# Reading a matmul's 256 moving columns by turns from its two halves, in a non-local block on one core

## The reference, cut to what matters

```python
q = jnp.einsum('bchw,dc->bdhw', x, theta_w) + theta_b[None, :, None, None]     # 256 planes
xpool = _maxpool2(x)                                                          # 2 x 2, 256 pixels
k = jnp.einsum('bchw,dc->bdhw', xpool, phi_w) + phi_b[None, :, None, None]
v = jnp.einsum('bchw,dc->bdhw', xpool, g_w) + g_b[None, :, None, None]
qk = jnp.einsum('bdn,bdm->bnm', q, k) * hp ** (-0.5)
p = jax.nn.softmax(qk, axis=-1)
vp = jnp.einsum('bdm,bnm->bdn', v, p)
out = jnp.einsum('bdhw,cd->bchw', vp, z_w) + z_b[None, :, None, None]
return out + x
```

## Time and profile before

| | us |
|---|---|
| median of 3 runs | 2043.75 (2041.75 to 2043.93) |
| profiled execution, first to last instruction | 2040.4 |
| TensorE matmul rows, busy | 2026.8 |
| TensorE weight loads, busy | 2024.5 |
| VectorE busy | 1558.1 |
| GpSimd busy | 1366.5 |
| ScalarE busy | 1300.0 |

### The profile page before, as it was taken

One profiled execution on the slowest core, in us unless ns is written; L12 is line 12 of the kernel. 1 busy time (PEld: TensorE's weight loads), 2 busy tenths in 40 slices (PEclk: granted clock), 3 DMA queues, 4 the chain that ended last, 5 costly groups with the idle time before them and its releaser, 6 DMA issues.

```text
span 2040.4 us, 48999 instructions
## 1 busy us (share of the span) xinstructions
PE 2026.8 (99%) x17790; PEld 2024.5 (99%) x17790; DVE 1558.1 (76%) x2625; ACT 1300.0 (64%) x2228; POOL 1366.5 (67%) x828
## 2 busy tenths in 40 slices
PE   9999999999999999999999999999999999999998
PEld 9999999999999999999999999999999999999998
DVE  8878777787777877777877778777787777787777
ACT  6666666666566665666666666666666566666663
POOL 4577666776666766667766677666677666776663
PEclk9999999999999999999999999999999999999999
DMA  7565656746556565566565664656656556656554
GB/s 243 191 212 184 213 169 214 236 170 210 175 207 232 180 210 185 186 226 210 181 212 171 215 237 169 209 177 207 232 180 210 184 187 226 209 182 214 170 193 166
DMA packets 213963, 407.27 MB, mean 200 GB/s; under 512 B 12720, under 2 KB 17840, under 8 KB 213936
## 3 DMA queue, kind: packets, MB, share of 16 engines
q1 hardware_dynamic: 213792, 406.90, 59.0%
q10 hardware_dynamic: 144, 0.01, 0.0%
HBM read 272.64 MB, written 134.22 MB: 199 GB/s over the span
## 4 chain that ended last, share of the span: by engine, by line
PE 97%; DVE 2%; POOL 0%; DMA 0%; issue 0%; ACT 0%; SPq 0%; DVEq 0%; POOLq 0%
PE bank L967 97%; DVE x_top L755 0%; DVE pt_raw L736 0%; DMA x<-x 0%; DVE x_bot L755 0%; DVE pooled L708 0%; POOL att_lo L631 0%; POOL x_split_lo L613 0%; POOL att_f L626 0%; DVE x L755 0%; PE bank L974 0%; SPq L265 0%; DVE q_lo L714 0%; ACT att_hi L425 0%; DVE xp_lo L851 0%
## 5 line engine op out<-in xcount | busy, mean ns | idle before, releaser
L613 POOL TENSOR_TENSOR x_split_lo<-x,x_split_hi 128x1024 fp32r<-128x1024 f32 x255 | 614.6, 2417 | 248.4 <-ACT x_split_hi L386 226.7
L967 PE MATMUL bank<-x_split_hi,theta_hi 128*128 128x256 f32 x2048 | 565.8, 276 | 3.1 <-POOL x_split_lo L613 2.0
L967 PE MATMUL bank<-x_split_lo,theta_hi 128*128 128x256 f32 x2048 | 565.7, 276 | 0.0
L967 PE MATMUL bank<-x_split_hi,theta_lo 128*128 128x256 f32 x2048 | 565.7, 276 | 0.0
L967 PE MATMUL bank<-att_hi,z_hi 128*128 128x256 f32 x1792 | 495.4, 276 | 3.6 <-DVE x_bot L755 2.5
L967 PE MATMUL bank<-att_hi,z_lo 128*128 128x256 f32 x1792 | 494.9, 276 | 0.0
L967 PE MATMUL bank<-att_lo,z_hi 128*128 128x256 f32 x1792 | 494.9, 276 | 0.0
L736 DVE STREAM_TRANSPOSE pt_raw<-probs 32x256 f32<-32x256 f32 x1024 | 445.9, 435 | 18.4 <-ACT probs L489 1.8
L631 POOL TENSOR_TENSOR att_lo<-att_f,att_hi 128x768 fp32r<-128x768 f32 x191 | 282.6, 1487 | 159.4 <-ACT att_hi L425 159.4
L967 PEld LDWEIGHTS bank<-x_split_hi,theta_hi 128*128 128x128 f32 x2048 | 384.6, 188 | 3.5 <-issue 3.5
L967 PEld LDWEIGHTS bank<-x_split_hi,theta_lo 128*128 128x128 f32 x2048 | 384.6, 188 | 0.0
(11 more groups left out here) (76 smaller groups left out, 4390.0 us busy)
## 6 DMA issues: line engine op xcount, KB each, us to landing
x<-x SPq DMA_DIRECT2D x258, 512.0 KB, 3.9
x_top<-x SPq DMA_DIRECT2D x128, 512.0 KB, 7.0
out<-x_top SPq DMA_DIRECT2D x128, 512.0 KB, 3.3
x_bot<-x SPq DMA_DIRECT2D x126, 512.0 KB, 5.2
out<-x_bot SPq DMA_DIRECT2D x126, 512.0 KB, 6.6
x_top<-theta_wt SPq DMA_DIRECT2D x4, 256.0 KB, 5.4
x_top<-g_wt SPq DMA_DIRECT2D x4, 256.0 KB, 5.4
x_bot<-z_wt SPq DMA_DIRECT2D x4, 256.0 KB, 6.2
```

Of the source, the lines that this page charges most:

```text
L613: nc.gpsimd.tensor_tensor(flat(lo), flat(x_chunk(s, c)), raw(flat(hi)), ALU.subtract).then_inc(x_ready, 1)
L967: last = nc.tensor.matmul(dst, stationary(a), moving(b), start=start and n == 0, stop=stop and n == len(PRODUCTS) - 1, skip_group_check=re ...
```

## The change

`product` hands the matmul its moving operand and its destination in another order of columns. The helper `woven` cuts 256 columns into two halves of 128 and each half into four runs of 32; the matmul takes the first run of the first half, the first run of the second half, the second run of the first half and so on. The destination's columns go in the same order, so each result stands where it stood. The stationary operand, the semaphores and all other engines' work are untouched, and `keep_busy` doesn't call it.

```diff
+            def woven(columns):
+
+                return columns.rearrange("p (half line c) -> p line half c", half=2, c=32)
+
             def product(dst, stationary, moving, start, stop, reopens=False):
 
                 for n, (a, b) in enumerate(PRODUCTS):
-                    last = nc.tensor.matmul(dst, stationary(a), moving(b), start=start and n == 0,
+                    last = nc.tensor.matmul(woven(dst), stationary(a), woven(moving(b)), start=start and n == 0,
                                             stop=stop and n == len(PRODUCTS) - 1, skip_group_check=reopens)
                 return last
```

## The result

The changed kernel takes 2128.86 us (median of 4 runs, 2127.85 to 2129.76) against 2043.47 (4 runs beside it, 2041.75 to 2043.93): a ratio of 1.0417, 95% interval 1.0402 to 1.0432. The forecast of 1964 us was on the wrong side, and the time lies above its range of 1960 to 2115.

The account below looks back on a forecast made before the run. TensorE's unbroken matmul line was taken to bound the kernel: 76.8 us saved in the steady stretch and 2.1 and 1.2 at the ends, together 80, giving 1964 us; range 1960 to 2115.

Parts of the forecast that it names:

- Jumps ... I take 0: Seven breaks per matmul in SBUF reads and seven in PSUM writes were costed at nothing, from ScalarE and VectorE rows.
- The sentence for the opposite case: Sign in the trace: a larger distance between matmul starts, the same in every group whatever the addresses, means breaks cost.
- The floor: Lowest distance between starts of 256-column matmuls, 109.2 ns, taken from the bf16 filler's 2.5 ns overhead.
- first "meeting" of 4.2 ns: Moving reads and the next weights' load supposedly meet in SBUF once per matmul, costing 4.2 ns; twice, 8.5 ns.
- the rival at 2036 us: Only the slower pace goes, 113.4 ns everywhere, saving 6.6 us and about 1 us; gains of 2036 to 1990 us: 0.12.
- No meeting saves them: Turned reads keep a constant distance from the weights' load, so the 4.2 and 8.5 ns per matmul go.
- The term of -76.8 us: Saving in the steady stretch: 16,764 matmuls going from 113.78 to 109.2 ns each.
- The picture behind it: Moving reads overtake the weights' load in SBUF addresses; in step at 192 bytes (`project_k` 448), they would not meet.
- The zero for the jumps on the SBUF side: Seven breaks in each matmul's moving read were taken as free.
- The rival "jumps cost": Each break loses column time: 2095 us at one column, 2147 at two; chances 0.08, and 0.14 including longer meetings.
- The rival of streams running together: Moving reads and weights' load meet and stay together, so every matmul takes 117.7 ns: 66 us more, 2110 us; chance 0.12.

Follow-up runs that it names:

- the groups: Kernel before the change, with groups of 48 extra matmuls at its end whose results nobody reads; only their own times count: contiguous fp32r 113.3 ns, by turns 118.7.

## Why the prediction was wrong

**What held.** TensorE bounds the kernel, and the distance of its starts is the whole result: +5.02 ns times 16,764 is 84.2 of 85.6 us. The other engines' idle time was cover enough, and the list of waits has no new row. "Jumps ... I take 0" held for PSUM's side, measured alone at 1.0008 [0.9997, 1.0019]. The Trainium skill, "PSUM — Partial Sum Buffer", Specifications, would have had matmuls with a non-contiguous pattern there slow down significantly; for runs of 128 bytes the measurement differs, and it decides. The sentence for the opposite case was also right: "if the distance is larger and the same in every group, whatever the addresses, the jumps cost". The distance is the same in every group, and it is the reads' breaks that cost.

**The floor (the first step that failed).** "For 256 columns that would be 106.7 + 2.5 = 109.2 ns" is true of bf16, measured at 109.2 with 256 columns, and false of fp32r. There a contiguous matmul has 6.7 ns above its columns at 128, 192 and 256 columns with a quarter of the weights (256 at every distance measured). So the first "meeting" of 4.2 ns, which was to be saved in 16,764 matmuls, doesn't go with the weights' load: the faster pace was the best one seen in any contiguous 256-column run of this type. As far as these runs show, what could be gained was the slower pace in `project_k`, 6.6 us and about 1 at the start (the rival at 2036 us).

**"No meeting saves them" (the step that decided).** The term of -76.8 us came out as +84.2 us. The picture behind it was half right. The weights' load does disturb the contiguous stream: in the groups the pace goes with the distance of the two modulo 256 bytes (113.3, 120.0, 117.8, 118.7 ns), and no longer does with a quarter of the weights. The Trainium skill's "TensorE: Matmul & The Clock Gate", Part 2, with two independent read ports and a load that steals nothing from the running matmul, isn't borne out by these rows for fp32r; bf16 shows no such thing at the one layout measured. But the turned reads have a price of their own, which the picture had no place for: 118.3 ns even with a quarter of the weights, against 113.3 in order, and 118.7 to 120.0 at all four distances. What they were to avoid was, at 192 bytes in the faster pace, already avoided.

**The zero for the jumps on the SBUF side** came from rows of ScalarE and VectorE, which say nothing of a moving read. The rival "jumps cost" had the right part of the change: the measured time lies between its 2095 us (one column's time each) and its 2147 (two). Its fixed price per jump is wrong: 3, 7 and 15 jumps cost 0, 5.5 and 6.7 ns, and seven jumps cost 4.5 to 6.7 by where they lead.

**The rival of streams running together**, 2110 us, is about as near as a number, by luck: it would have had the distance decide. At a distance of 128 bytes its loss is larger and at none is it gone.

**What stays open.** Why fp32r reads in broken order are slower even with few weights, when bf16 isn't (a bf16 column is half the bytes; whether the type or the bytes decide wasn't tested); why runs of 64 are free in the whole kernel and cost 3 to 5 ns in groups alone; why 512 columns have more than twice the excess of 256; and what makes one distance hold two paces, which a filler flips. At 64 bytes the whole kernel had stretches at 113.3 that the groups at that distance never show, so the table of distances isn't all of it. A layout or hand-over that keeps all calls, `project_k` too, in the faster pace wasn't found; no kernel here was faster than the one before.

## What to carry to other kernels

Where TensorE bounds, read the distance of the starts call by call, and look for calls of one shape at two paces before thinking of what limits them. A floor measured in one type or pattern isn't one for another: a group of 48 matmuls alone, in the same type, shows in one run what an order or an address costs. Leave fp32r's moving operand contiguous, and choose the distance between moving columns and weights by measurement, since 64 bytes cost up to 6% in a group alone and 1.5% in the whole kernel here.

## What was not expected of the hardware

- In groups alone, the pace of contiguous fp32r matmuls with 128 x 128 weights goes with the distance between moving columns and weights modulo 256 bytes: 113.3 ns at 192 bytes (117.8 in its slower pace), 120.0 at 0, 117.8 at 64, 118.7 at 128. With 32 columns of weights it is 113.3 at all of them.
- A pace is a state: one filler matmul ahead of `project_k` gave it 113.4 ns in place of 117.7, and the 504 other matmuls of an image 117.8 in place of 113.4; the whole kernel took about 63 us more.
- bf16 pays 2.5 ns over its columns in any order measured (82.5 ns for 192 columns, 109.2 for 256); fp32r pays 6.7 in order (128 to 256 columns), and 11 to 13 for 256 columns broken into runs of 32.
- One contiguous fp32r matmul with 512 columns takes longer than two with 256: 231.1 against 226.7 ns with 32 columns of weights, 233.1 against 226.7 with 128.
